# Down product ahead of the up product in each slot of a fused scan and mixture-of-experts layer

## Chip, cores and metric

One core of one Trainium2 chip runs the whole kernel in one launch. The metric is device time in microseconds (us). The engines are called PE (TensorE), DVE (VectorE), ACT (ScalarE), POOL (GpSimd) and SP (SyncE, which issues most DMAs); PEld is TensorE's loading of weights, which overlaps its matmuls.

## What is computed

A layer on x of shape (2, 2048, 128): a layer norm, then the input plus a selective state-space scan with 16 states per feature, plus a feed-forward part with 64 gated experts and one shared expert. The feed-forward part is what the change touches:

```python
def relu2(x):
    return jnp.square(jax.nn.relu(x))
...
tidx, tw = _route(xf, router_w, correction_bias)      # top 8 of 64 experts, by groups
combine = zeros((T, E)).at[arange(T)[:, None], tidx].add(tw)

def body(acc, ew):
    wu, wd, c = ew
    return (acc + c[:, None] * (relu2(xf @ wu) @ wd), None)
routed, _ = jax.lax.scan(body, zeros_like(xf), (up_w, down_w, combine.T))
shared = relu2(xf @ shared_up_w) @ shared_down_w
return routed + shared
```

Each expert has an inner width of 64, so two experts fill 128 partitions; the shared expert has an inner width of 256, which is two times 128. The scan runs over time as `h = dA*h + dB*x`, its norm is limited, and `y = sum(h*C)`.

## The kernel before

**Chunks and slots.** The 4096 tokens are cut into 8 chunks (`NCH`) of 512 columns (`CT`), written c = 0 to 7 here. A chunk has 34 slots (`SLOTS`): slots 0 and 1 are the shared expert's two halves (`SHP` = 2), slots 2 to 33 are the 32 pairs of experts. Every engine has its own program, written out by hand in slot order and tied to the others by semaphores; an engine takes its instructions strictly in the order in which they are written. No scheduler decides anything.

**One slot's chain.** PE makes the up product U of the slot (function `three`, three matmuls, lines 1038 to 1040) in one of two banks, `U[slot % 2]`. DVE takes `relu` of it times the gate (`mul`, L885; L889 for the shared expert) into one of two `relu` buffers, and counts `gated_done`. ACT squares that into `act` (`square`, L715), one of four buffers (`ABUFS`), and counts `sq_done`. PE multiplies `act` by the down weights and accumulates in bank DN (`down_mm`, L1088, two matmul records for each), and counts `down_done`. The waits are:

- U(s) needs relu(s-2), since it writes the bank that relu(s-2) reads (`wait_read`).
- relu(s) needs U(s), and act(s-2), since it overwrites the buffer that act(s-2) reads.
- act(s) needs relu(s), and the down product of s-4.
- DN(s) needs act(s). The first one of a chunk, DN(0), also needs ACT's copy of the finished DN of the chunk before (`dn_copy`, L719).

**What else runs in the slots.** For the scan, each pair of slots has one of the 16 states: ACT makes the decay (L685, L691), POOL multiplies b_rows (L537), DVE scans (L944) on odd slots and multiplies by C (`ymul`, L897) on even slots, POOL adds to `yacc` (L546), ACT squares the state to `hsq` (L707), and PE sums four of these at slots 2, 12, 20 and 28 (`norms`, bank GR, L1094). Spread over the slots of chunk c, `prep(c + 1, slot)` prepares the next chunk: POOL's layer norm `xn` (L444), PE's transposes of it (L1044, slot 4, called T below), ACT's `x_hi`, DVE's `x_lo`, PE's projections (slots 6 and 10), a transpose (slot 8), ACT's exponential `sig` (L620), DVE's `reciprocal` (L823), POOL's `sfc` (L492), DVE's `max` (L831), and at slot 26 PE's transposes of the gates. At slot 19 PE transposes the finished output of chunk c-1 (`out_mm`).

**PE's slot.** The order within a slot is: the wait and U, then a down product three slots back, then `norms`, `out_mm` and `prep` where the slot has them:

```python
wait_read(pe, c, slot - 2)
...three(U[slot % 2][:, :], up_hi[:, w], up_lo[:, w], par(c)).then_inc(up_done, 1)
if 3 < slot:
    down_mm(c, slot - 3)
elif slot < 3 and not first:
    down_mm(c - 1, SLOTS - 3 + slot)
```

In slot 3 the down product DN(0) stands further below, after the norms.

Of the kernel before, what the change touches and what calls it, by code (L numbers as in the profile page):

```python
# [42 lines left out]
def layer_program(nc, x_in, wdt_in, bdt_in, wb_in, wc_in, alog_in, dp_in, rw_in, cbias_in,  # L43
# [10 lines left out]
    PAIRS = E // 2  # L54
    SHP = SH // P
    SLOTS = PAIRS + SHP
    QUARTERS = 4
# [33 lines left out]
    with ExitStack() as ctx:  # L91
# [3 lines left out]
        def sem(name):  # L95
            return ctx.enter_context(nc.semaphore(name))
# [99 lines left out]
        w_down = [sem(f"w_down{q}") for q in range(QUARTERS)]  # L196
# [39 lines left out]
        def wait(eng, s, value):  # L236

            if not isinstance(value, int) or value > 0:
                eng.wait_ge(s, value)
# [9 lines left out]
        def act_at(c, slot):  # L249
            return act[:, (c * SLOTS + slot) % ABUFS, :]  # L250
# [8 lines left out]
        def par(c):  # L259
            return bass.ds((c % 2) * CT, CT)  # L260
# [28 lines left out]
        def wait_read(eng, c, slot):  # L289


            wait(eng, gated_done, c * SLOTS + slot + 1)
# [741 lines left out]
        def _(pe):  # L1034
            mm = nc.tensor.matmul

            def three(dst, hi, lo, cols, start=True, stop=True):
                mm(dst, hi, x_hi[:, cols], start=start, stop=False)  # L1038
                mm(dst, hi, x_lo[:, cols], start=False, stop=False)  # L1039
                return mm(dst, lo, x_hi[:, cols], start=False, stop=stop)  # L1040
# [12 lines left out]
            def prep(pc, slot):  # L1053
                if slot == 4:
                    pe.wait_ge(xn_ready, pc + 1)
                    if pc > 0:
                        pe.wait_ge(gate_ready, pc)
                    transposes(lambda k: xn[:, k, :]).then_inc(xt_done, 1)
                if slot == 6:
                    pe.wait_ge(xlo_ready, pc + 1)  # L1060
                    three(M[0:E + 2 * N, :], proj_hi[:, 1, 0:E + 2 * N], proj_lo[:, 1, 0:E + 2 * N], par(pc)).then_inc(lg_done, 1)
                if slot == 8:
                    pe.wait_ge(lg_copied, pc + 1)
                    pe.wait_ge(bc_ready, pc + 1)
                    alone(pe)
                    for k in range(KB):
                        i = nc.tensor.transpose(M[:, k * E:(k + 1) * E], logit[0:E, k * P:(k + 1) * P], ident[0:E, 0:E])
                    i.then_inc(lgt_done, 1)
                if slot == 10:
                    pe.wait_ge(sig_exp, pc + 1)  # L1070
                    alone(pe)
                    three(M[:, :], proj_hi[:, 0, :], proj_lo[:, 0, :], par(pc)).then_inc(z_done, 1)
                if slot == 26:
                    pe.wait_ge(cc_ready, pc + 1)
                    pe.wait_ge(z_copied, pc + 1)
                    if pc > 1:
                        pe.wait_ge(res_ready, pc - 1)
                    for k in range(KB):
                        i = nc.tensor.transpose(M[0:E, k * P:(k + 1) * P], cc[:, k, :], ident[:, :])
                    i.then_inc(ct_done, 1)  # L1080

            def down_mm(c, slot):
                s = c * SLOTS + slot
                pe.wait_ge(sq_done, s + 1)
                if slot == 0:
                    wait(pe, dn_copied, c)
                w = sdown[:, slot, :] if slot < SHP else down[:, slot - SHP, :]
                mm(DN[:, :], w, act_at(c, slot), start=slot == 0, stop=slot == SLOTS - 1).then_inc(down_done, 1)  # L1088
# [7 lines left out]
            def norms(c, group):  # L1096
                for n in range(group * NB, (group + 1) * NB):
                    norm(c, n)

            def chunk(c, first, last):  # L1100
                for slot in range(SLOTS):
                    if slot == 0:
                        pe.wait_ge(xlo_ready, c + 1)
                    pair = slot - SHP
                    if first and pair >= 0 and pair % (PAIRS // QUARTERS) == 0:
                        pe.wait_ge(up_split, pair // (PAIRS // QUARTERS) + 1)
                    wait_read(pe, c, slot - 2)
                    if pair >= 0:
                        w = slice(pair * P, (pair + 1) * P)
                        three(U[slot % 2][:, :], up_hi[:, w], up_lo[:, w], par(c)).then_inc(up_done, 1)  # L1110
                    else:
                        w = slice(slot * P, (slot + 1) * P)
                        three(U[slot % 2][:, :], sup_hi[:, w], sup_lo[:, w], par(c)).then_inc(up_done, 1)
                    if 3 < slot:
                        if first and pair >= 3 and (pair - 3) % (PAIRS // QUARTERS) == 0:
                            pe.wait_ge(w_down[(pair - 3) // (PAIRS // QUARTERS)], 32)
                        down_mm(c, slot - 3)
                    elif slot < 3 and not first:
                        down_mm(c - 1, SLOTS - 3 + slot)
                    if slot == 2 and not first:  # L1120
                        norms(c - 1, N // NB - 1)
                    if slot > 2 * NB + 2 and slot % (2 * NB) == 4:
                        norms(c, slot // (2 * NB) - 1)
                    if slot == 3:
                        down_mm(c, 0)
                    if slot == 19 and not first:
                        out_mm(c - 1)
                    if not last:
                        prep(c + 1, slot)

            def out_mm(c):
                pe.wait_ge(ot_ready, c + 1)
                if c == NCH - 1:
                    pe.wait_ge(res_ready, c)
                elif c == NCH - 2:
                    pe.wait_ge(gate_ready, NCH)
                else:
                    pe.wait_ge(z_copied, c + 3)
                transposes(lambda k: ot[:, k * P:(k + 1) * P]).then_inc(ot_done, 1)
# [4 lines left out]
            pe.wait_ge(dve_init, 3)  # L1144
            pe.wait_ge(w_sdown, 16)
            chunk(0, True, False)
            for c in range(1, NCH - 1):
                chunk(c, False, False)
            chunk(NCH - 1, False, True)
            norms(NCH - 1, N // NB - 1)  # L1150
            for slot in (3, 2, 1):
# [38 lines left out]
```

## Time and profile before

| | |
|---|---|
| median of 3 runs | 572.5 us (572.01 to 573.7) |
| profiled execution: its time | 574.56 us |
| profiled execution: its span | 572.8 us |
| PE busy | 508.6 us, 89% |
| DVE busy | 496.0 us, 87% |
| ACT busy | 470.4 us, 82% |
| POOL busy | 469.3 us, 82% |
| mean granted clock of TensorE | 0.998 |

The engines are nearly equally busy, so no share of the span tells which of them sets the pace; it has to be read stretch by stretch, from the idle time in brackets that stands behind an instruction and from what ended it. A matmul's end is modelled in the records, so PE's pace is read from the distance between starts.

### The profile page before, as it was taken

How to read it: one execution, taken by the hardware profiler on the slowest of the kernel's cores; microseconds unless marked ns; L12 is line 12 of the kernel's file. 1: busy time of each engine (PE TensorE's matmuls, PEld its weight loads, DVE VectorE, ACT ScalarE, POOL GpSimd, SP SyncE). 2: the span in 40 equal slices, each digit the busy share in tenths (PEclk: the TensorE clock that was granted, in tenths of full speed). 3: DMA queues.
4: the chain of work that ended last, by engine and by line, in shares of the span. 5: the costliest groups of instructions: out<-in, count | busy, mean ns of one | idle time of the engine just before them, and what ended most of it. 6: DMA issues, size and time to landing. Idle time of an engine off the chain costs nothing.

```text
span 572.8 us, 7918 instructions
## 1 busy us (share of the span) xinstructions
PE 508.6 (89%) x1666; PEld 278.0 (49%) x1666; DVE 496.0 (87%) x1158; ACT 470.4 (82%) x922; POOL 469.3 (82%) x430
## 2 busy tenths in 40 slices
PE   2158899998898988999899998999989998999996
PEld 1034445554454545565455544555445554555552
DVE  3657899899988899899998899888998899979984
ACT  2768798799886998888986998879988889988872
POOL 2389898897888979897988978889897979968762
PEclk9999999999999999999999999999999999999999
DMA  8956865887869877987678877697769877699951
GB/s 200 326 166 229 277 258 197 318 291 259 247 191 348 276 261 232 347 271 262 247 239 307 304 264 248 197 364 264 272 216 321 300 249 246 219 318 353 317 189 37
DMA packets 65649, 149.32 MB, mean 261 GB/s; under 512 B 14048, under 2 KB 31040, under 8 KB 65600
## 3 DMA queue, kind: packets, MB, share of 16 engines
q1 hardware_dynamic: 63728, 147.07, 76.3%
q10 hardware_dynamic: 1872, 1.75, 0.9%
q14 instruction: 36, 0.29, 0.2%
q8 instruction: 13, 0.21, 0.1%
HBM read 143.03 MB, written 5.77 MB: 260 GB/s over the span
## 4 chain that ended last, share of the span: by engine, by line
POOL 28%; issue 22%; DVE 18%; PE 14%; ACT 8%; DMA 8%; SPq 1%; POOLq 1%; DVEq 0%; ACTq 0%
POOL yacc L546 10%; DMA bc_rows<-bc_dram 7%; PE DN L1088 7%; POOL bc_rows L537 6%; DVE DC L944 4%; DVE relu L885 4%; POOL xn L444 3%; DVE g L831 3%; DVE bc_rows L897 3%; PE U L1038 2%; PE U L1039 2%; PE U L1040 2%; ACT act L715 2%; POOL rstd L438 1%; POOL rest L527 1%
## 5 line engine op out<-in xcount | busy, mean ns | idle before, releaser
L1088 PE MATMUL DN<-act,down 128*128 128x512 f32 x512 | 261.9, 593 | 1.9 <-ACT act L715 1.9
L715 ACT ACTIVATE act<-relu 128x512 f32<-128x512 f32 x272 | 169.5, 623 | 44.6 <-DVE relu L885 38.3
L885 DVE SCALAR_TENSOR_TENSOR relu<-U,gate_rows 128x512 f32<-128x512 f32 x256 | 173.6, 678 | 34.0 <-PE U L1040 17.8
L546 POOL TENSOR_TENSOR yacc<-yacc,bc_rows 128x512 f32<-128x512 f32 x120 | 154.5, 1287 | 44.9 <-DVE bc_rows L897 44.9
L1038 PE MATMUL U<-x_hi,up_hi 128*128 128x512 f32 x256 | 163.4, 638 | 23.5 <-DVE relu L885 22.5
L537 POOL TENSOR_TENSOR bc_rows<-dtx_all,bc_rows 128x512 f32<-128x512 f32 x128 | 164.4, 1285 | 20.2 <-DMA bc_rows<-bc_dram 20.2
L944 DVE TENSOR_TENSOR_SCAN DC<-DC,carry,bc_rows 128x512 f32<-128x512 f32 x96 | 122.7, 1278 | 0.0
L1088 PEld LDWEIGHTS DN<-act,down 128*128 128x128 f32 x512 | 95.3, 188 | 28.7 <-ACT act L715 6.6
L1038 PEld LDWEIGHTS U<-x_hi,up_hi 128*128 128x128 f32 x256 | 48.2, 188 | 113.7 <-DVE relu L885 70.1
L1039 PE MATMUL U<-x_lo,up_hi 128*128 128x512 f32 x256 | 101.2, 395 | 0.0
L1040 PE MATMUL U<-x_hi,up_lo 128*128 128x512 f32 x256 | 101.1, 395 | 0.0
L685 ACT ACTIVATE DC<-dt_all,a 128x512 f32<-128x512 f32 x128 | 88.1, 688 | 8.2 <-ACT gate L669 0.7
L897 DVE TENSOR_TENSOR bc_rows<-DC,bc_rows 128x512 f32<-128x512 f32 x120 | 81.3, 678 | 0.0
L691 ACT ACTIVATE DC<-DC 128x512 f32<-128x512 f32 x128 | 74.4, 581 | 5.2 <-ACT gate L669 4.3
L707 ACT ACTIVATE hsq<-DC 128x512 bf16<-128x512 f32 x128 | 74.3, 581 | 0.0
L1039 PEld LDWEIGHTS U<-x_lo,up_hi 128*128 128x128 f32 x256 | 48.6, 190 | 31.0 <-issue 30.3
L1040 PEld LDWEIGHTS U<-x_hi,up_lo 128*128 128x128 f32 x256 | 48.2, 188 | 11.1
L944 DVE TENSOR_TENSOR_SCAN DC<-DC,bc_rows 128x512 f32<-128x512 f32 x32 | 39.0, 1219 | 0.6 <-ACT DC L691 0.6
L1094 PE MATMUL GR<-hsq,ones_bf 128*1 128x512 bf16 x128 | 32.8, 378 | 0.0
L831 DVE MAX8 g<-sfc 128x8 f32<-128x8 f32 x256 | 19.5, 153 | 5.2 <-POOL sfc L492 5.2
L1094 PEld LDWEIGHTS GR<-hsq,ones_bf 128*1 128x1 bf16 x128 | 8.0, 82 | 32.8 <-issue 19.7
L444 POOL TENSOR_SCALAR xn<-xs,mv,rstd 128x128 f32<-128x128 f32 x28 | 22.0, 800 | 1.5 <-POOL rstd L438 1.5
(113 smaller groups left out, 501.5 us busy)
## 6 DMA issues: line engine op xcount, KB each, us to landing
bc_rows<-bc_dram SPq DMA_DIRECT2D x128, 512.0 KB, 6.0
gate_rows<-gate_dram SPq DMA_DIRECT2D x128, 512.0 KB, 4.8
xs<-in_L_attn_x SPq DMA_DIRECT2D x8, 256.0 KB, 5.6
down<-in_L_ffn_down_w SPq DMA_DIRECT2D x8, 256.0 KB, 4.9
xr<-in_L_attn_x SPq DMA_DIRECT2D x8, 256.0 KB, 5.6
rest_kept_dram<-rest SPq DMA_DIRECT2D x8, 256.0 KB, 4.3
out<-res SPq DMA_DIRECT2D x8, 256.0 KB, 4.5
dtx_all<-in_L_ffn_up_w SPq DMA_DIRECT2D x3, 512.0 KB, 5.6
```

The source lines that it names most:

```text
L537: g.tensor_tensor(b, dtx_all[:, sl(c)], b, ALU.mult).then_inc(dbp_done, 1)
L546: g.tensor_tensor(yacc[:, :], yacc[:, :], c_rows[:, (c * N + n) % BUFS, :], ALU.add).then_inc(yacc_done, 1)
L685: a.activation(state_bank(c, n), dt_all[:, sl(c)], ACT.Tanh, scale=a16[:, n:n + 1]).then_inc(tanh_done, 1)
L691: a.activation(state_bank(c, n), state_bank(c, n), ACT.Exp, scale=16.0).then_inc(exp_done, 1)
L715: a.activation(act_at(c, slot), relu[:, slot % 2, :], ACT.Square).then_inc(sq_done, 1)
L885: v.scalar_tensor_tensor(out=relu[:, slot % 2, :], in0=U[slot % 2][:, :], scalar=0.0, in1=gate_rows[:, k // 2 % SBUFS, slot % 2, :], op0=A ...
L897: v.tensor_tensor(dst, state_bank(c, n), c_rows[:, (c * N + n) % BUFS, :], ALU.mult).then_inc(ym_done, 1)
L944: v.tensor_tensor_scan(state_bank(c, n), state_bank(c, n), b_rows[:, (c * N + n) % BUFS, :], initial, ALU.mult, ALU.add).then_inc(scan_don ...
L1038: mm(dst, hi, x_hi[:, cols], start=start, stop=False)
L1039: mm(dst, hi, x_lo[:, cols], start=False, stop=False)
L1040: return mm(dst, lo, x_hi[:, cols], start=False, stop=stop)
L1088: mm(DN[:, :], w, act_at(c, slot), start=slot == 0, stop=slot == SLOTS - 1).then_inc(down_done, 1)
```

## The change

In each slot PE now issues the down product three slots back ahead of the wait for the relu, and U behind it:

```diff
@@ -1104,6 +1104,12 @@
                     pair = slot - SHP
                     if first and pair >= 0 and pair % (PAIRS // QUARTERS) == 0:
                         pe.wait_ge(up_split, pair // (PAIRS // QUARTERS) + 1)
+                    if 3 < slot:
+                        if first and pair >= 3 and (pair - 3) % (PAIRS // QUARTERS) == 0:
+                            pe.wait_ge(w_down[(pair - 3) // (PAIRS // QUARTERS)], 32)
+                        down_mm(c, slot - 3)
+                    elif slot < 3 and not first:
+                        down_mm(c - 1, SLOTS - 3 + slot)
                     wait_read(pe, c, slot - 2)
                     if pair >= 0:
                         w = slice(pair * P, (pair + 1) * P)
@@ -1111,12 +1117,6 @@
                     else:
                         w = slice(slot * P, (slot + 1) * P)
                         three(U[slot % 2][:, :], sup_hi[:, w], sup_lo[:, w], par(c)).then_inc(up_done, 1)
-                    if 3 < slot:
-                        if first and pair >= 3 and (pair - 3) % (PAIRS // QUARTERS) == 0:
-                            pe.wait_ge(w_down[(pair - 3) // (PAIRS // QUARTERS)], 32)
-                        down_mm(c, slot - 3)
-                    elif slot < 3 and not first:
-                        down_mm(c - 1, SLOTS - 3 + slot)
                     if slot == 2 and not first:
                         norms(c - 1, N // NB - 1)
                     if slot > 2 * NB + 2 and slot % (2 * NB) == 4:
```

No instruction is added or removed, and the programs of DVE, ACT, POOL and SP are the same. What moves on PE is shown at two places of chunk 1 (chunks 2 to 6 repeat it).

PE before, from U of slot 3 to the two products of slot 5 (the x4 row is T, the transposes for the next chunk, in slot 4):

```order
L1038 MATMUL U<-x_hi,up_hi 128x512
L1039 MATMUL U<-x_lo,up_hi 128x512
L1040 MATMUL U<-x_hi,up_lo 128x512
L1088 MATMUL DN<-act,sdown 128x512
L1038 MATMUL U<-x_hi,up_hi 128x512
L1039 MATMUL U<-x_lo,up_hi 128x512
L1040 MATMUL U<-x_hi,up_lo 128x512
L1088 MATMUL DN<-act,sdown 128x512
L1044 MATMUL M<-ident,xn 128x128 x4
L1038 MATMUL U<-x_hi,up_hi 128x512
L1039 MATMUL U<-x_lo,up_hi 128x512
```

PE after the change, at the same place:

```order
L1038 MATMUL U<-x_hi,up_hi 128x512
L1039 MATMUL U<-x_lo,up_hi 128x512
L1040 MATMUL U<-x_hi,up_lo 128x512
L1088 MATMUL DN<-act,sdown 128x512 x2
L1038 MATMUL U<-x_hi,up_hi 128x512
L1039 MATMUL U<-x_lo,up_hi 128x512
L1040 MATMUL U<-x_hi,up_lo 128x512
L1044 MATMUL M<-ident,xn 128x128 x4
L1088 MATMUL DN<-act,down 128x512
L1038 MATMUL U<-x_hi,up_hi 128x512
L1039 MATMUL U<-x_lo,up_hi 128x512
```

Ahead of T the same work is done in both, with DN(0) and DN(1) now side by side; behind T, U of slot 5 used to come at once, and now DN(2) comes first.

PE before, from the down product of slot 18 through slot 19, whose own down product is DN(16), to the U of slot 20 (the x4 row is `out_mm`):

```order
L1088 MATMUL DN<-act,down 128x512
L1038 MATMUL U<-x_hi,up_hi 128x512
L1039 MATMUL U<-x_lo,up_hi 128x512
L1040 MATMUL U<-x_hi,up_lo 128x512
L1088 MATMUL DN<-act,down 128x512
L1044 MATMUL M<-ident,ot 128x128 x4
L1038 MATMUL U<-x_hi,up_hi 128x512
L1039 MATMUL U<-x_lo,up_hi 128x512
```

PE after, from the down product of slot 19, DN(16), to the U of slot 20:

```order
L1088 MATMUL DN<-act,down 128x512
L1038 MATMUL U<-x_hi,up_hi 128x512
L1039 MATMUL U<-x_lo,up_hi 128x512
L1040 MATMUL U<-x_hi,up_lo 128x512
L1044 MATMUL M<-ident,ot 128x128 x4
L1088 MATMUL DN<-act,down 128x512
L1038 MATMUL U<-x_hi,up_hi 128x512
L1039 MATMUL U<-x_lo,up_hi 128x512
```

The down product that stands between U(18) and U(19) was DN(15) and is now DN(16); between U(19) and U(20) it was DN(16) and is now DN(17), behind the transposes. The same holds for every neighbouring pair of slots: U(s), DN(s-3), U(s+1) became U(s), DN(s-2), U(s+1).

## Rows read from the trace of the kernel before

**Rows 1.** The page's head: span and instructions.

```profile
span 572.8 us, 7918 instructions
```

**Rows 2.** Windows: slots 4 to 12 of chunk 3 (PE, PEld, DVE, ACT, POOL busy).

```profile
246.80:262.00 15.20, 15.20 (x56) 9.37 (x55) 14.29 (x21) 13.52 (x26) 15.20 (x13) 1.00 0.87 286
```

**Rows 3.** Waits of the whole run: total us, times, longest.

```profile
PEld U L1038 <- DVE relu L885: 70.1, 71, 2.4
...
DVE sig L823 <- ACT sig L620: 7.7, 8, 3.4
...
PE M L1044 <- POOL xn L444: 6.1, 5, 2.4
```

**Rows 4.** Timeline: xn and T in chunk 3, and T in chunk 0.

```profile
244.29 3.15 POOL L444 TENSOR_SCALAR xn<-xs,mv,rstd 128x128 f32<-128x128 f32 x4 [0.24 <-POOL rstd L438]
...
247.64 0.60 PE L1044 MATMUL M<-ident,xn 128*128 128x128 f32 x4
...
45.93 0.66 PE L1044 MATMUL M<-ident,xn 128*128 128x128 f32 x4 [2.43 <-POOL xn L444]
```

**Rows 5.** Timeline: PE at slots 7 and 8 of chunk 3; PEld in the tail.

```profile
252.57 1.02 PE L1088 MATMUL DN<-act,down 128*128 128x512 f32 x2
...
254.13 1.02 PE L1088 MATMUL DN<-act,down 128*128 128x512 f32 x2
...
564.22 0.19 PEld L1088 LDWEIGHTS DN<-act,down 128*128 128x128 f32 x1 [0.24 <-issue]
...
565.08 0.19 PEld L1088 LDWEIGHTS DN<-act,down 128*128 128x128 f32 x1 [0.24 <-issue]
```

**Rows 6.** Timeline: U(9), relu(9) and the reciprocal of chunk 3.

```profile
256.03 0.39 PE L1040 MATMUL U<-x_hi,up_lo 128*128 128x512 f32 x1
...
256.46 0.69 DVE L885 SCALAR_TENSOR_TENSOR relu<-U,gate_rows 128x512 f32<-128x512 f32 x1 [0.19 <-PE U L1040]
...
258.11 0.96 DVE L823 RECIPROCAL sig<-sig 128x64 f32<-128x64 f32 x2 [0.36 <-ACT sig L620]
```

**Rows 7.** Timeline: DVE's waits in chunk 0 (two) and chunk 1.

```profile
56.67 0.96 DVE L823 RECIPROCAL sig<-sig 128x64 f32<-128x64 f32 x2 [0.57 <-ACT sig L620]
...
65.50 0.65 DVE L831 MAX8 g<-sfc 128x8 f32<-128x8 f32 x8 [2.46 <-POOL sfc L492]
...
124.23 0.96 DVE L823 RECIPROCAL sig<-sig 128x64 f32<-128x64 f32 x2 [0.88 <-ACT sig L620]
```

**Rows 8.** Timeline of chunk 3: U(18), U(19), act(16), DN(16), relu(18), relu(19).

```profile
272.60 0.50 PE L1038 MATMUL U<-x_hi,up_hi 128*128 128x512 f32 x1
...
274.93 0.50 PE L1038 MATMUL U<-x_hi,up_hi 128*128 128x512 f32 x1 [0.52 <-DVE relu L885]
...
275.45 0.62 ACT L715 ACTIVATE act<-relu 128x512 f32<-128x512 f32 x1
...
276.12 1.12 PE L1088 MATMUL DN<-act,down 128*128 128x512 f32 x2 [0.23 <-ACT act L715]
...
276.20 0.69 DVE L885 SCALAR_TENSOR_TENSOR relu<-U,gate_rows 128x512 f32<-128x512 f32 x1 [0.63 <-ACT act L715]
...
278.10 0.69 DVE L885 SCALAR_TENSOR_TENSOR relu<-U,gate_rows 128x512 f32<-128x512 f32 x1
```

**Rows 9.** Timeline: the last norms of the program, which wait for hsq.

```profile
562.73 0.52 PEld L1094 LDWEIGHTS GR<-hsq,ones_bf 128*1 128x1 bf16 x4 [0.76 <-ACT hsq L707]
```

**Rows 10.** Timeline: successive matmuls of one U, at 35 us and at 46 us.

```profile
35.28 0.63 PE L1039 MATMUL U<-x_lo,sup_hi 128*128 128x512 f32 x1
35.70 0.63 PE L1040 MATMUL U<-x_hi,sup_lo 128*128 128x512 f32 x1
...
46.65 0.39 PE L1039 MATMUL U<-x_lo,up_hi 128*128 128x512 f32 x1
46.88 0.40 PE L1040 MATMUL U<-x_hi,up_lo 128*128 128x512 f32 x1
```

**Rows 11.** Timeline: relu(3) of chunk 3.

```profile
245.43 0.69 DVE L885 SCALAR_TENSOR_TENSOR relu<-U,gate_rows 128x512 f32<-128x512 f32 x1 [0.57 <-PE U L1040]
```

## Prediction, made before the changed kernel was run

> **What bounds the kernel now.** I read the waits of the whole run first, then the timeline of one middle chunk (chunk 3) engine by engine, and compared the other chunks with it; chunks 1 to 6 repeat each other within a few tenths of a microsecond. Two stretches alternate. In slots 26 to 14 of the next chunk, PE has no gap: slots 4 to 12 of chunk 3 show it busy for 15.20 of 15.20 us [rows 2]. In slots 15 to 25 DVE has the routing work of the next chunk on top of its own, and PE waits for it; most of the 70.1 us for which U's weights wait for a relu is there [rows 3]. The seam between a chunk and its preparation is T, the transposes of xn. POOL finishes xn at 247.44 (244.29 + 3.15), and T starts at 247.64 [rows 4]. T is held by POOL in 5 of the 7 chunks that have it, for 6.1 us in all [rows 3], and in the other two by less than PE's own work.
>
> **What the change does, and what it does not.** PE executes a fixed sequence, so what counts is what stands between two instructions that wait. In the steady state that is unchanged: between U(s) and U(s+1) stands one down product, before and after. When PE is stopped by a relu, it resumes with the same U and has the same work up to the next U, so the down product that was "done while waiting" is no gain: the next one takes its place. The change is that this product is now DN(s-2), not DN(s-3), and that everything PE does at a slot's end (norms, T, projections, out_mm) now stands one down product earlier relative to the U stream. That gives four places to cost.
>
> Prices first. Slot 8's down product starts 1.56 us after slot 7's (254.13 - 252.57), and one U and one DN lie between the starts [rows 5]. In the tail the weight loads of consecutive halves are 0.43 apart (0.86 over two, 564.22 to 565.08), so a DN costs 0.86 and a U 0.70 [rows 5].
>
> **Place 1: T.** Ahead of T PE does the same work in both kernels less one DN (from the previous chunk on), so it arrives at T 0.86 earlier. That buys nothing, because xn isn't there: T starts when xn ends, at most about 0.1 earlier in the two chunks where PE was the later one (247.64 against 247.44 plus a hand-over). Behind T, however, DN(2) now comes ahead of U(5). So U(5), U(6) and all U's of this PE-bound stretch come 0.86 later than before. The projections don't, since they moved ahead by the same 0.86: x_hi, x_lo and ACT's sig keep their times.
>
> Does DVE notice? Relu(5) comes after x_lo and has slack, relu(6) some, relu(7) none. At relu(9) DVE is visibly waiting: U(9)'s last matmul starts at 256.03, and relu(9) 0.43 later at 256.46 behind 0.19 of idle [rows 6]. So relu(9) moves by the whole 0.86. But two operations on, DVE waits for ACT's sig, by 0.36 in chunk 3 and 0.88 in chunk 1 [rows 6, 7], and sig does not move. That wait swallows its part. Over the run it is 7.7 us in 8 times; without the longest (3.4, the first preparation) and chunk 0 (0.57) it is 3.73 us over six chunks [rows 3, 7]. Chunk 0 costs nothing at all, as it waits 2.46 us for POOL at the max behind it [rows 7]. The sum: 6 x 0.86 = 5.16, less 0.2 for the two earlier T's, less 3.73, is 1.2 us. Behind the reciprocal DVE is the bound up to slot 25, its relu starts the loads for the next chunk's rows, POOL's chain to the next xn starts from these, and so what is lost stays lost. Bounds: 0 if DVE has more slack than I read, 5.0 if sig moves along with the relus ahead of it on ACT.
>
> **Place 2: DN(16) ahead of U(19).** ACT reaches act(16) late, at 275.45, and it ends at 276.07; DN(16) started at 276.12 before, when U(19) at 274.93 was already made [rows 8]. Now DN(16) starts at the same 276.12 and U(19) only 0.86 behind, at 276.98: 2.05 later than before. U(19) is over at 277.68, its last matmul starts 0.23 ahead of that, and a relu can follow that start by 0.43: 277.88. Relu(19) ran at 278.10, since relu(18) itself had to wait for act(16) and a scan lies between the two [rows 8]. So a margin of 0.2 us is left, and the stall costs nothing. It does not grow: in slots 20 to 24 DVE has the slower work, and by U(24) PE waits for a relu again. I take 0. Lower bound 0, as nothing gets earlier here; upper bound, if the margin is overrun by as much as it is wide, 0.2 x 7 = 1.4. Elsewhere the act that DN now needs ends before U(s) does, by 0.1 where PE and ACT start from the same relu (U takes 0.70, act 0.62) and by more in the PE-bound stretch.
>
> **Place 3: the chunk's start.** DN(33) of the chunk before now precedes U(2), and no DN stands between U(2) and U(3). So U(3) comes 0.86 earlier, and relu(3) loses its 0.57 of idle [rows 11]. But DN(0) and DN(1) follow together, U(4) is where it was, and DVE waits there for that instead. ACT copies DN earlier and then waits longer for T. I take 0; if all 0.57 were kept in six chunks it would be a gain of 3.4.
>
> **Place 4: the end.** Behind U(33) of the last chunk one DN less is left, 0.86. But the norms wait for the last hsq, which releases them at 562.73 [rows 9]; PE would wait there instead. Gain 0.1 of at most 0.86; I take 0.1.
>
> **Sum.** +1.2 + 0 + 0 - 0.1 = +1.1 us, 0.2%. The profiled execution has a span of 572.8 us [rows 1] and a time of 574.56; on that the sum gives 575.7; the runs shown have a median of 572.5, 2.1 lower, and I put it on that: 573.6 us. A measurement of this kernel tells about 0.3% (1.7 us) from no change, so this is "no change that can be measured", on the slow side.
>
> **The rivals.**
>
> - *Forecast: the late U's are mostly swallowed by the wait for sig.* 573.6, within 571.8 and 575.4. For it: the repeated wait of rows 6 and 7. Chance 0.45.
> - *Nothing at all changes.* The same work in the same cyclic order, and slack at relu(5) to relu(9) that is larger than it looks. 572.5. Against it: the idle ahead of relu(9). Chance 0.14.
> - *The delay of U behind T is paid in full (slower).* It decides if ACT gets to sig later too, because it waits for act(7) or act(8) first, or if the loads for the next chunk come later by more than DVE does. Then 0.86 in six chunks, 5.0: 577.5. Against it: in chunk 3 the release of the reciprocal is ACT, not DVE [rows 6], so ACT is behind on its own account. Chance 0.20.
> - *DN(16) bites (slower).* It decides where U(19) is later than 277.88 + 0.2. Each microsecond beyond costs 7 in the run; 0.5 us too late gives 3.5: 577.1 with the forecast's own part. Chance 0.09.
> - *TensorE's clock falls in the new gap (slower).* PE now stands from the end of U(18), 272.60 + 0.70 = 273.3, to 276.12 [rows 8]: 2.8 us, where it waited in two pieces before. At 35 us, early in the program, matmuls were 0.42 apart; at 46 us, right behind an idle of 2.43 us, 0.23 [rows 4, 10]. That is 1.2 GHz against 2.4 GHz; 2.43 us did not lower it. A slot at half speed costs about 1.5 us more; for two slots in seven chunks, less the slack, some 15 us: 588. Chance 0.04. The Trainium skill (TensorE: Matmul & The Clock Gate, "Part 1: The HAM clock gate") says that the slow state is the default and that activity releases it, an idle stretch bringing it back; by that rule this change, which joins two waits into one, is a step towards it. The trace agrees that there are these two speeds; that a gap of 2.8 us is enough, no run here shows.
> - *Faster.* The earlier relu(3), the earlier copy of DN and the earlier norms reach POOL's chain to xn. 3.4 + 0.9: 568.5. Against it: xn ends where POOL's own chain and its loads put it. Chance 0.08.
>
> **How the numbers follow.** The time is the forecast's, 573.6. The range goes up to 577.6, so as to hold the full payment, and down to 571.4, below the case of nothing; outside are the clock, most of the faster case and the far ends of the rest, under 0.2 together. The forecast's own range is 571.8 to 575.4. Slower by over 0.3% (above 574.2): 0.20 + 0.08 + 0.04 of the slow cases and about 0.10 of the forecast's upper part, 0.42. Faster (below 570.8): 0.07. The same: 0.51.
>
> **What would show it.** Right: behind T a DN row, then U(5); x_hi, x_lo and sig at unchanged distance from T; the idle ahead of the reciprocal gone or cut from 0.3 to 0.9 us to near 0; PE's wait for POOL at T up by about 0.86 in each chunk (6.1 us to some 11); new rows of DN waiting for act in slot 19, some 2.5 us each; relu(19) without idle; relu(3) without its 0.57. Wrong: idle ahead of relu(19) or relu(20) caused by U; a stretch of matmuls 0.42 apart; the distance from T to T in a middle chunk grown by 0.86 or unchanged, or shorter.

## The result, and the profile after

The changed kernel takes 580.7 us (579.9 to 582.61, 4 runs) against 572.58 us before on the same chip: a ratio of 1.0144, 95% interval 1.0114 to 1.0174. It is 8.1 us slower, outside the range that I gave. The page of the changed kernel, its head and the two PE groups that moved:

```profile
span 578.5 us, 7918 instructions
...
PE 514.5 (89%) x1666; PEld 285.7 (49%) x1666; DVE 495.7 (86%) x1158; ACT 471.0 (81%) x922; POOL 469.1 (81%) x430
...
L1088 PE MATMUL DN<-act,down 128*128 128x512 f32 x512 | 272.1, 614 | 17.8 <-ACT act L715 17.8
...
L1038 PE MATMUL U<-x_hi,up_hi 128*128 128x512 f32 x256 | 195.9, 765 | 5.7 <-DVE relu L885 4.8
```

The instructions are as many as before. But the same 512 down matmuls are now busy for 272.1 us, 614 ns each, where the page of the kernel before has 261.9 us and 593 ns, and the first matmul of a U takes 765 ns, before 638. About half of the one and most of the other come with the new order: number 3 below, which has it in 32 of 34 slots, shows 604 and 739 ns with half clock behind T in chunk 0 alone. The sign that something else changed is the clock that TensorE was granted, as a share of its full 2.4 GHz; half clock, 1.2 GHz, is the lower of its two levels. The mean granted clock is 0.973 to 0.979 in the four runs of the changed kernel. It was 0.998 in the profiled execution before, and 0.991 to 0.999 in all but one of the runs of the kernel before that ran beside the first experiments.

The waits of the changed kernel (total us, times, longest), to be held against [rows 3]:

```profile
PEld U L1038 <- DVE relu L885: 42.3, 81, 1.7
...
DVE relu L885 <- PE U L1040: 19.9, 35, 1.6
...
PE DN L1088 <- ACT act L715: 17.8, 7, 2.6
...
PE M L1044 <- POOL xn L444: 7.7, 6, 3.0
...
DVE sig L823 <- ACT sig L620: 3.3, 1, 3.3
```

As forecast, U's wait for the relu shrinks (70.1 to 42.3) and a wait of DN for act appears, seven times, one for each chunk with a preparation, 2.5 us each. And DVE's wait for sig, 7.7 us before, is gone but for the first preparation. PE's wait for xn at T is 7.7 us, where I had some 11.

**Behind T.** The timeline of chunk 3 of the changed kernel, T to the reciprocal, to be held against [rows 4, 6]:

```profile
253.47 0.66 PE L1044 MATMUL M<-ident,xn 128*128 128x128 f32 x4 [0.38 <-POOL xn L444]
...
262.79 0.39 PE L1040 MATMUL U<-x_hi,up_lo 128*128 128x512 f32 x1
...
263.22 0.69 DVE L885 SCALAR_TENSOR_TENSOR relu<-U,gate_rows 128x512 f32<-128x512 f32 x1 [0.19 <-PE U L1040]
263.55 0.42 ACT L620 ACTIVATE sig<-sig 128x256 f32<-128x256 f32 x1
264.42 0.95 DVE L823 RECIPROCAL sig<-sig 128x64 f32<-128x64 f32 x2
```

From T to relu(9) it is 9.75 us; before it was 256.46 - 247.64 = 8.82. The 0.9 arrives in full. The reciprocal starts 10.95 behind T, before 10.47, and has no idle ahead of it. This is Place 1 as predicted, with one difference: x_lo starts 2.12 us behind T (before 1.80), where I had it unchanged; sig keeps its time, 9.57 (before 9.52).

**Slots 18 to 20.** The timeline of chunk 3, to be held against [rows 8]:

```profile
278.90 0.50 PE L1038 MATMUL U<-x_hi,up_hi 128*128 128x512 f32 x1
...
281.74 0.62 ACT L715 ACTIVATE act<-relu 128x512 f32<-128x512 f32 x1
...
282.41 1.13 PE L1088 MATMUL DN<-act,down 128*128 128x512 f32 x2 [2.55 <-ACT act L715]
...
283.61 0.55 PE L1039 MATMUL U<-x_lo,up_hi 128*128 128x512 f32 x1
...
283.96 0.63 PE L1040 MATMUL U<-x_hi,up_lo 128*128 128x512 f32 x1
...
284.62 0.69 DVE L885 SCALAR_TENSOR_TENSOR relu<-U,gate_rows 128x512 f32<-128x512 f32 x1 [0.24 <-PE U L1040]
...
285.23 1.92 PE L1088 MATMUL DN<-act,down 128*128 128x512 f32 x2
```

And the same place in chunk 4 of the same execution:

```profile
346.41 0.50 PE L1038 MATMUL U<-x_hi,up_hi 128*128 128x512 f32 x1
...
349.92 1.12 PE L1088 MATMUL DN<-act,down 128*128 128x512 f32 x2 [2.55 <-ACT act L715]
...
351.11 0.39 PE L1039 MATMUL U<-x_lo,up_hi 128*128 128x512 f32 x1
...
351.34 0.39 PE L1040 MATMUL U<-x_hi,up_lo 128*128 128x512 f32 x1
...
351.95 0.69 DVE L885 SCALAR_TENSOR_TENSOR relu<-U,gate_rows 128x512 f32<-128x512 f32 x1
```

Both chunks have the wait of 2.55 us and the late U(19). In chunk 4, U's last two matmuls are 0.23 apart and relu(19) comes without idle: the margin of 0.2 us that I had worked out is there. In chunk 3 they are 0.35 apart, the DN behind them takes 1.92 instead of 1.02, and relu(19) waits for U. The windows of the changed kernel (length, then busy time of PE, PEld, DVE, ACT and POOL), right behind the wait in chunk 3 and in chunk 4 (the third column from the end is the granted clock):

```profile
282.70:286.20 3.50, 3.50 (x12) 2.16 (x11) 3.26 (x7) 3.42 (x9) 3.30 (x5) 0.64 0.81 287
...
350.30:354.00 3.70, 3.70 (x16) 2.08 (x15) 3.58 (x7) 3.59 (x11) 3.50 (x5) 1.00 0.73 279
```

So TensorE fell to 1.2 GHz for some 3 us in the one and stayed at 2.4 GHz in the other. What it costs is seen from relu(16) to relu(26), a stretch in which DVE sets the pace; its ends in chunk 3 of the kernel before:

```profile
271.88 0.67 DVE L885 SCALAR_TENSOR_TENSOR relu<-U,gate_rows 128x512 f32<-128x512 f32 x1
...
292.18 0.68 DVE L885 SCALAR_TENSOR_TENSOR relu<-U,gate_rows 128x512 f32<-128x512 f32 x1
```

And in chunks 3 and 4 of the changed kernel:

```profile
278.18 0.67 DVE L885 SCALAR_TENSOR_TENSOR relu<-U,gate_rows 128x512 f32<-128x512 f32 x1
...
299.85 0.67 DVE L885 SCALAR_TENSOR_TENSOR relu<-U,gate_rows 128x512 f32<-128x512 f32 x1
...
345.68 0.67 DVE L885 SCALAR_TENSOR_TENSOR relu<-U,gate_rows 128x512 f32<-128x512 f32 x1
...
365.86 0.68 DVE L885 SCALAR_TENSOR_TENSOR relu<-U,gate_rows 128x512 f32<-128x512 f32 x1
```

That is 21.67 and 20.18 us; before it was 20.30 and 20.17. I took the same two distances, T to relu(16) and relu(16) to relu(26), in all chunks. "Half clock" marks the chunks with matmuls about 0.42 apart in that stretch:

| chunk | T to relu(16), before | after | relu(16) to relu(26), before | after |
|---|---|---|---|---|
| 0 | 26.50 | 27.34, half clock behind T | 19.60 | 21.28, half clock |
| 1 | 24.78 | 24.69 | 20.35 | 21.58, half clock |
| 2 | 24.79 | 26.36, half clock behind T | 20.35 | 21.66, half clock |
| 3 | 24.24 | 24.71 | 20.30 | 21.67, half clock |
| 4 | 24.38 | 24.58 | 20.17 | 20.18 |
| 5 | 24.51 | 24.75 | 20.35 | 21.66, half clock |
| 6 | 24.51 | 24.72 | 20.36 | 20.36 |

The sum of the last two columns' differences is 6.9 us, and it is made by the five chunks with half clock. In chunk 0, 0.3 of the 1.7 us are not the clock's: numbers 3 and 4 below take 19.90 there at full clock. The first pair adds 3.4 us, of which 2.4 are the two half-clock stretches behind T (in chunks 0 and 2). The way from relu(33) to the next T was 3.8 us shorter in all in this execution; I did not trace what sets it, and it differs by 2 us from chunk to chunk in the kernel before too (9.51 to 11.30). With 0.8 less at the end (Place 4), these add up to 5.7 us, the difference of the two profiled spans (578.5 and 572.8); the medians differ by 8.1.

### The profile page after: what moved, and what is told of

It reads as the page before. It is cut to its first block, busy times and chain, and to the rows that moved or that the text cites. A ratio compares the mean times of both kernels' runs of the same rounds, so it can differ in the third digit from the quotient of the medians.

```text
span 578.5 us, 7918 instructions
## 1 busy us (share of the span) xinstructions
PE 514.5 (89%) x1666; PEld 285.7 (49%) x1666; DVE 495.7 (86%) x1158; ACT 471.0 (81%) x922; POOL 469.1 (81%) x430
## 4 chain that ended last, share of the span: by engine, by line
PE 15%; POOL 12%; issue 9%; DVE 7%; DMA 3%; ACT 3%; SPq 1%; POOLq 0%; DVEq 0%; ACTq 0%
PE DN L1088 8%; POOL yacc L546 5%; DMA bc_rows<-bc_dram 3%; POOL bc_rows L537 3%; PE U L1038 2%; PE U L1039 2%; PE U L1040 2%; DVE DC L944 2%; DVE relu L885 2%; POOL xn L444 1%; DVE bc_rows L897 1%; DVE g L831 1%; PE GR L1094 1%; ACT act L715 1%; POOL ot L518 1%
## 5 line engine op out<-in xcount | busy, mean ns | idle before, releaser
L1088 PE MATMUL DN<-act,down 128*128 128x512 f32 x512 | 272.1, 614 | 17.8 <-ACT act L715 17.8
L1038 PE MATMUL U<-x_hi,up_hi 128*128 128x512 f32 x256 | 195.9, 765 | 5.7 <-DVE relu L885 4.8
L1088 PEld LDWEIGHTS DN<-act,down 128*128 128x128 f32 x512 | 92.1, 192 | 52.2 <-ACT act L715 24.3
L1039 PE MATMUL U<-x_lo,up_hi 128*128 128x512 f32 x256 | 102.9, 402 | 0.0
L1040 PE MATMUL U<-x_hi,up_lo 128*128 128x512 f32 x256 | 102.4, 400 | 0.0
L1038 PEld LDWEIGHTS U<-x_hi,up_hi 128*128 128x128 f32 x256 | 49.5, 193 | 88.3 <-issue 44.5
L1079 PE MATMUL M<-ident,cc 128*64 128x128 f32 x32 | 5.3, 290 | 15.5 <-POOL cc L487 15.5
```

## The experiments

Each kernel differs in the slots that have the new order (down product first); the others have the old one. The edit to the kernel before is this, with another `EARLY` in each:

```diff
+            EARLY = range(18, 26)
...
+                    if slot in EARLY:
+                        ...the down product of slot - 3
                     wait_read(pe, c, slot - 2)
...
-                    if 3 < slot:
+                    if slot not in EARLY:
+                        ...the down product of slot - 3
```

Theory A is the clock. Theory B puts the loss behind T. Theory C, added from number 5 on, is the lateness of U(19) by itself. Numbers 1 to 4, 5 to 8, 9 to 11 and 12 ran on four chips, each group beside runs of the kernel before with medians of 572.99, 572.3, 572.42 and 573.03 us; a ratio is always to these. Between groups the ratios are the safer comparison.

**1. The new order in slots 18 to 25 alone** (`EARLY = range(18, 26)`).

> The kernel before, with the new order (down product first) in slots 18 to 25 alone. Theory A (the clock: the joined wait ahead of DN(16) lets TensorE fall to half clock in most chunks, some 1.3 us each): 5 to 9 us slower than before, half-speed matmuls right behind the wait, relu(16) to relu(26) longer by about 1.3 us in the chunks that have them and unchanged in the others. Theory B (the loss is made elsewhere, behind T, and the wait is covered by DVE's work): within 1.5 us of before.

Measured: 576.07 us, ratio 1.0044 (1.0016 to 1.0073). So this part alone makes the kernel slower, by 3 us and not by the 5 to 9 of Theory A; the interval (0.9 to 4.2 us) does not shut out the 1.5 us that Theory B allowed either. The profiled execution shows what happens. Chunk 3 of it:

```profile
275.95 1.12 PE L1088 MATMUL DN<-act,down 128*128 128x512 f32 x2 [1.96 <-ACT act L715]
...
277.24 0.63 PE L1039 MATMUL U<-x_lo,up_hi 128*128 128x512 f32 x1
277.66 0.63 PE L1040 MATMUL U<-x_hi,up_lo 128*128 128x512 f32 x1
...
278.33 0.69 DVE L885 SCALAR_TENSOR_TENSOR relu<-U,gate_rows 128x512 f32<-128x512 f32 x1 [0.41 <-PE U L1040]
```

PE's wait is only 1.96 us here (DN(14) and DN(15) both stand ahead of U(18) where the old order meets the new), and 3 of 7 chunks had half clock behind it. These three took 21.67 to 21.69 us from relu(16) to relu(26), the other four what they took before, to 0.3 us. In all chunks relu(26) to relu(33) was some 0.35 us shorter, which may hide a part of the loss. The ten runs go from 572.68 us (clock 0.993) to 580.87 (clock 0.979), so the number of chunks at half clock most likely differs from execution to execution.

**2. The new order in slots 5 to 14 alone** (`EARLY = range(5, 15)`).

> The kernel before, with the new order in slots 5 to 14 alone, so that a down product stands between T and U(5), and PE gets to T when it did before. Theory A: +1.2 us, since the wait for sig swallows most of the 0.86 us a chunk. Rival (the delay behind T is paid in full and makes most of the loss): +5 us or more.

Measured: 573.77 us against 572.99, ratio 1.0017 (0.9994 to 1.004). T to relu(9) was 9.68 to 9.81 us in every chunk (before 8.82 to 8.95), and T to relu(16) of chunks 3 to 6 24.60 to 24.75 (before 24.24 to 24.51); in chunks 0 to 2 it was no longer than before. The delay is there and mostly swallowed, 0.8 us of 5.2. The rival, payment in full, is out: the interval ends at 2.3 us.

**3. The change without slots 18 and 19** (`EARLY` = all slots but 18 and 19).

> The changed kernel, with the old order (U first) in slots 18 and 19 alone, so that U(19) is made inside the wait for act(16) again. Theory A: 5 to 8 us faster than the changed kernel, so 573 to 576; half-speed stretches left only where T waits long for xn. Theory B: within 2 us of the changed kernel's 580.7.

Measured: 573.79 us, ratio to before 1.0013 (0.9996 to 1.0031). Putting two slots back takes away 6.9 of the 8.1 us (by the ratios, 1.0144 and 1.0013, 7.5). Relu(16) to relu(26) is 20.18 to 20.37 in chunks 1 to 6. Theory B is out. There was still half clock behind T in chunk 0.

**4. The change, with idle matmuls in the gap.** They write bank M, which nobody reads before it is written again, so the output is the same:

```diff
+                    if slot == 19 and not last:
+                        pe.wait_ge(z_copied, c + 2)
+                        for i in range(FILL):
+                            mm(M[:, :], up_hi[:, 0:P], x_hi[:, par(c)], start=True, stop=True)
                     if slot in EARLY:
```

> The changed kernel, with 8 idle matmuls of 128x512 (0.23 us each, 1.9 us, into bank M, which nobody reads before it is written again) ahead of DN(16) in slot 19 of chunks 0 to 6. They add work and change no wait. Theory A: the clock holds, and the kernel is 5 to 8 us faster than the changed one, 573 to 576, with relu(19) at the same distance from act(16) as before. Theory B: the same as the changed kernel or slower by the part that reaches past act(16).

Measured, with 8 of them: 576.5 us (573.07 to 581.14), ratio 1.0057 (1.0026 to 1.0088), mean clock of the runs 0.987 to 0.994; just above the 573 to 576 expected. Chunk 3 of the profiled execution:

```profile
273.71 2.00 PE L1113 MATMUL M<-x_hi,up_hi 128*128 128x512 f32 x8
...
276.44 1.12 PE L1088 MATMUL DN<-act,down 128*128 128x512 f32 x2 [0.73 <-ACT act L715]
...
277.63 0.39 PE L1039 MATMUL U<-x_lo,up_hi 128*128 128x512 f32 x1
277.86 0.39 PE L1040 MATMUL U<-x_hi,up_lo 128*128 128x512 f32 x1
...
278.41 0.69 DVE L885 SCALAR_TENSOR_TENSOR relu<-U,gate_rows 128x512 f32<-128x512 f32 x1
```

DN(16) starts when act(16) is done, as in the changed kernel, and U(19) is as late. But TensorE had work until shortly before, the matmuls behind keep 0.23, relu(19) has no idle, and relu(16) to relu(26) is back to 20.18 to 20.37 in chunks 1 to 6. Adding 56 matmuls of no use made the kernel 4.2 us faster, and the interval lies wholly below the changed kernel's (1.0114 to 1.0174). No account of the loss by order and waits alone can do that.

**5. The new order in slot 19 alone** (`EARLY = (19,)`).

> The kernel before, with the new order in slot 19 alone: U(18), DN(15), DN(16), U(19). U(19) is as late as in the changed kernel, behind the wait for act(16), but DN(15) lies in front of that wait and shortens it to about 2.0 us. Theory A (the clock makes the loss, the lateness of U(19) by itself is covered): within 1 us of before, no half-speed matmuls in slots 19 to 21, relu(19) without idle caused by U. Theory C (the lateness is paid): 1.5 to 3 us slower than before with a full clock.

Measured: 572.82 us against 572.3, ratio 1.0008 (0.9994 to 1.0023). Its wait ahead of DN(16), and what follows, in chunk 3:

```profile
277.17 1.13 PE L1088 MATMUL DN<-act,down 128*128 128x512 f32 x2 [1.70 <-ACT act L715]
...
278.59 0.40 PE L1040 MATMUL U<-x_hi,up_lo 128*128 128x512 f32 x1
...
279.15 0.69 DVE L885 SCALAR_TENSOR_TENSOR relu<-U,gate_rows 128x512 f32<-128x512 f32 x1
```

U(19) stands behind DN(16) as in the changed kernel, no chunk has half clock there, and no loss can be told. Theory C is out: at full clock the lateness is covered. Half clock did come behind T in chunk 2 of this execution, though the order there is the old one.

**6. The change, with 4 idle matmuls** (`FILL = 4`).

> The changed kernel, with 4 idle matmuls (0.93 us) instead of 8 ahead of DN(16). Theory A: the remaining wait is about 1.7 us, the fill can't reach past act(16) even at half speed, and the kernel is as fast as or faster than with 8: 573.5 to 576, with less spread. Theory C: 1.5 to 3 us above the changed kernel without slots 18 and 19 (573.8), at the same clock.

Measured: 575.04 us (572.86 to 577.0), ratio 1.0042 (1.002 to 1.0064), 5.7 below the changed kernel and with less spread than with 8. The wait left ahead of DN(16) is 1.63 to 1.66 us. Both filled kernels stay above number 3 (573.79, ratio 1.0013), by 1.2 and 2.7 us, the first within the intervals. Their profiled executions do not show where: neither has half clock in slots 16 to 26. Fill matmuls that fall into half clock themselves would take twice as long and push DN(16) back, more so with 8; but no profiled execution caught it, so this stays open.

**7 and 8. The cover behind T taken away.** In both, DVE's first two reciprocals, which wait for sig, stand behind relu(10); number 7 is otherwise the kernel before, number 8 has the new order in slots 5 to 14:

```diff
-            RECIP_AT = {10: [0, 1], 11: [2, 3]}
+            RECIP_AT = {10.5: [0, 1], 11: [2, 3]}
```

> The kernel before, with DVE's first two reciprocals behind relu(10) instead of ahead of it, so that DVE doesn't stand still for ACT's sig ahead of relu(10). Where the wait for sig is on the path, 1 to 2 us faster than before (0.1 us in a chunk such as chunk 3, where U(10) is ready only just then, up to 0.5 us in chunk 1). Rival (POOL's sfc or the next xn decides anyway): the same as before.

> The kernel with the new order in slots 5 to 14 alone, and the reciprocals behind relu(10). If it is the wait for sig that swallowed most of the 0.86 us per chunk behind T, it is taken away here and the delay is paid in full: 4 to 5 us slower than the kernel before with the reciprocals moved. If something else covers it, the difference is 1 us as it was without moving them.

Measured: number 7 570.87 us, ratio 0.9989 (0.9975 to 1.0004); number 8 576.69 us, ratio 1.0087 (1.0058 to 1.0115). The difference is 5.8 us, somewhat more than the 4 to 5 expected, where it is 0.8 with the reciprocals in their place. Over T to relu(16) of all chunks the two profiled executions differ by 5.2 us. Chunk 3 of number 8, relu(9), relu(10) and the reciprocal:

```profile
258.74 0.69 DVE L885 SCALAR_TENSOR_TENSOR relu<-U,gate_rows 128x512 f32<-128x512 f32 x1 [0.19 <-PE U L1040]
...
260.35 0.69 DVE L885 SCALAR_TENSOR_TENSOR relu<-U,gate_rows 128x512 f32<-128x512 f32 x1 [0.32 <-issue]
260.95 0.95 DVE L823 RECIPROCAL sig<-sig 128x64 f32<-128x64 f32 x2
```

There is nothing left to swallow the delay: T to relu(16) is 25.01 to 25.09 in chunks 3 to 6, in number 7 24.12 to 24.25, so 0.84 to 0.90 each. The wait for sig was the cover.

**9. The change without both places** (`EARLY` = slots 0 to 4, 15 to 17, 20 to 33).

> The changed kernel, with the old order in slots 18 and 19 and in slots 5 to 14; the new order is left in slots 0 to 4, 15 to 17 and 20 to 33. If the two places found so far are all, within 1 us of the kernel before (and 0.5 to 1 us faster than the change without 18 and 19 alone). If the earlier arrival at T costs by itself, because PE then stands longer ahead of it and the clock falls there in some chunks, 1 to 2.5 us slower than before.

Measured: 572.29 us, ratio 0.9999 (0.998 to 1.0017). Without the two places no loss is left that can be told. Half clock behind T (chunks 0 and 2 of the profiled execution, the latter 0.7 us longer from T to relu(16) than before) is there here too, without a loss in the median; what makes up for it I did not trace.

**10. Number 7 again, with more runs.**

> The kernel before with DVE's first two reciprocals behind relu(10), once more with more runs. The first time 1.4 us faster, with an interval that touched no change; expected 0.8 to 2 us faster, with an interval clear of it.

Measured: 571.52 us, ratio 0.9992 (0.9977 to 1.0006). The 0.8 to 2 us with an interval clear of 1 is missed. Taken by itself, moving the reciprocals is no gain that can be told.

**11. The changed kernel again.**

> The changed kernel once more, beside the two above: 579 to 583 us, a mean clock of 0.97 to 0.98, and half-speed matmuls behind DN(16) in four to six of the seven chunks, not always the same ones, with relu(16) to relu(26) longer by some 1.3 us there and nowhere else.

Measured: 580.84 us (577.65 to 583.95), clock 0.972 to 0.981, ratio 1.0134 (1.0107 to 1.0162). Half clock behind DN(16) in six of seven chunks, this time in chunk 4 too; these took 21.22 to 21.69 us from relu(16) to relu(26), and chunk 6, without it, 20.36.

**12. A version from the parts that did not hurt**: the new order in slots 20 to 25 and the reciprocals behind relu(10).

> The kernel before, with the new order in slots 20 to 25 alone and the reciprocals behind relu(10). In the run with the new order in slots 18 to 25 the stretch from relu(26) to relu(33) was 0.35 us shorter in each chunk, since no down product lies between U(25) and U(26) where PE becomes the bound. Without slots 18 and 19 there is no long wait and no half clock. If relu(33) is what the next chunk waits for: 2.4 us faster for it and 1 us for the reciprocals, 569 to 570.5 us. If the next chunk's start hangs on the loads that relu(25) releases, 33 to T grows by the same 0.35 and only the 1 us of the reciprocals is left, 571 to 572 us.

Measured: 571.08 us against 573.03, ratio 0.9973 (0.9954 to 0.9993): 2.0 us faster than the kernel before by the medians (1.5 by the ratio) and 9.6 below the changed one's 580.7. Relu(26) to relu(33) takes 11.26 to 11.39 us in chunks 0 to 6 (before 11.62 to 11.71). That is what I had expected for the case that the next chunk's start hangs on the loads. How much each of the two parts gives is not shown: the new order in slots 20 to 25 was not run alone, and the interval overlaps those of numbers 7 and 10.

## Why the prediction was wrong

- **The order of work** was read rightly. PE does the same between U(s) and U(s+1), and nothing is gained by filling the wait for the relu: that wait fell by 28 us in the changed kernel, and by 20 (70.1 to 49.9) in number 9, which is at 0.9999.
- **Place 1, behind T: right.** Its 0.86 appears at relu(9) in every chunk (number 2), the wait for sig swallows most of it (0.8 us left; I had 1.2), and with the wait gone it is paid in full, 5.2 us by the profiled executions and 5.8 by the medians, for my bound of 5.0 (numbers 7 and 8). The 0.2 us for the two chunks where PE was late at T is there too: T starts 0.06 behind xn, before 0.13 and 0.19.
- **Place 2, DN(16) ahead of U(19): this is the step that failed.** "So a margin of 0.2 us is left, and the stall costs nothing." That holds at full clock (chunk 4 above; number 5: 1.0008). But PE's idle ahead of DN(16), 2.55 us in one piece, is followed by half clock in five or six of seven chunks. A U with matmuls 0.42 to 0.43 apart takes some 1.28 instead of 0.70 (an estimate, three times that distance), and the row of the DN behind it shows 1.92 instead of 1.02; a margin of 0.2 doesn't cover that, and 1.2 to 1.4 us are paid each time. Five times, with the 0.3 of chunk 0, are the 6.9 us of the table; number 3, which takes the gap away, gets as much back in the medians, and that the two agree to the decimal is luck. Two of my signs of being wrong were there: idle ahead of relu(19) caused by U, and a stretch of matmuls 0.42 apart. I had this rival, with a chance of 0.04. The only measure I gave for it was one wait of 2.43 us that was followed by full clock [rows 4, 10], and one sample is no bound: in the changed kernel 2.55 us was followed by either speed. I overpriced it as well, 15 us for two slots in each of seven chunks, where some 3 us at half clock in five cost 7.
- The Trainium skill (TensorE: Matmul & The Clock Gate, "HAM oscillation — how this bites in real kernels") tells of idle between bursts of matmuls after which each burst starts at the lower clock. I had weighed the part on the two states only. The trace agrees with it in part: the granted clock is 0.64 in the 3.5 us behind the wait of chunk 3, but 1.00 behind the same wait of chunk 4.
- **Ahead of T.** I said that arriving 0.86 earlier "buys nothing"; that it could cost was not in the text. PE waits longer there in one piece: 2.58 us in chunk 2 of the changed kernel (before 1.63), with half clock behind it. The order is not needed for that: numbers 5 and 12, which have the old one at T, each show it once, behind 2.10 and 2.38 us. In the profiled execution the two such stretches lengthened T to relu(16) by 2.4 us more than the order alone. Over many runs the cost is small: numbers 3 and 9, which have it, are at 1.0013 and 0.9999.
- **Place 3, the chunk's start: right.** Relu(3) lost its 0.57 of idle, and relu(4) had 1.01 instead of 0.32.
- **Place 4, the end: mis-sized.** From relu(33) of the last chunk to DVE's final addition it was 4.58 us before and is 3.80: 0.8 gained, where I had 0.1. The first three of the four last norms don't need the last hsq, and ran while it was made.
- **A slip in the sums.** The "faster" rival's 3.4 + 0.9 below 572.5 is 568.2, not 568.5; nothing hangs on it.

## What to carry to other kernels

When a reordering joins two short waits of TensorE into one longer one, ask about the clock behind it, not only about who waits for the late product: at half clock a margin worked out at full clock is worth nothing. Here two slots of 34 made most of the loss (6.9 of 8.1 us); putting the independent U back into the gap took these 6.9 away, and idle matmuls in it 4.2 to 5.7. And where another engine's wait swallows a delay, name that wait and keep it in mind: an "improvement" that removes it (number 7) makes the delay visible (number 8).

## What had not been expected of the hardware

- The same wait in the same place is followed by half clock in some chunks and not in others of one execution. PE's idle ahead of DN(16) and the chunks with half clock behind it, in the profiled executions: 2.55 us, 5 of 7 and again 6 of 7; 1.96 us (number 1), 3 of 7; 1.70 us (number 5), 1.63 to 1.66 us (number 6) and 0.73 us (number 4), none of 7 each. The length of the wait alone does not decide it. Ahead of T, 2.10 us in chunk 2 of number 5 was followed by half clock, and 2.93 us in chunk 2 of number 3 by full clock:

```profile
181.52 0.66 PE L1044 MATMUL M<-ident,xn 128*128 128x128 f32 x4 [2.10 <-POOL xn L444]
...
182.25 0.63 PE L1039 MATMUL U<-x_lo,up_hi 128*128 128x512 f32 x1
182.68 0.63 PE L1040 MATMUL U<-x_hi,up_lo 128*128 128x512 f32 x1
```

```profile
182.22 0.66 PE L1044 MATMUL M<-ident,xn 128*128 128x128 f32 x4 [2.93 <-POOL xn L444]
...
183.80 0.39 PE L1039 MATMUL U<-x_lo,up_hi 128*128 128x512 f32 x1
184.03 0.40 PE L1040 MATMUL U<-x_hi,up_lo 128*128 128x512 f32 x1
```

What else decides it the runs don't show.

- A stretch at half clock behind DN(16) is short (some 3 us; the clock is back while PE works on), and costs 1.2 to 1.4 us here. Behind T in chunk 0 of the changed kernel it lasts some 6 us, from 45.85 to 51.7.
- The mean granted clock follows the count: 0.972 to 0.981 for the changed kernel, 0.988 to 0.993 without slots 18 and 19. A difference of 0.02 in it is some 23 us of the span at half clock, twice what a glance at "0.98" suggests: at half clock for 0.04 of the span it has lost 0.02.
- The granted clock does not show every stretch. In the kernel before, the matmuls at 35 us are 0.42 apart [rows 10], and the window over them has a granted clock of 1.00 (third column from the end), so the distance of the matmuls is the surer sign:

```profile
30.00:38.00 8.00, 4.94 (x13) 3.24 (x13) 3.56 (x12) 5.24 (x8) 7.55 (x9) 1.00 0.18 50
```
